# Routed expert outputs added into memory by accumulating indirect DMAs, and the shared expert moved into the routing stage

## The reference

```
scores  = sigmoid(x @ gate_w.T)                       # 2048 tokens, 16 experts
chosen  = top 4 of (scores + expert_bias) per token
weights = scores of the chosen, divided by their sum
routed  = sum over the chosen of weight * swiglu_e(x) # silu(x@wg.T) * (x@wu.T) @ wd.T, inner width 256
shared  = swiglu_shared(x)                            # for every token, weight 1
out     = layernorm(x + routed + shared)
```

## Time and profile before

| | |
|---|---|
| median of 3 runs | 1644.0 us (1643.52 to 1646.49) |
| profiled execution | span 1642.0 us, from its first to its last instruction; no time of its own is given beside it, and the median is 2.0 us above it |
| `route` | about 986 to 1056 us |
| `routed_experts` | about 1056 to 1514 us |
| `combine` | about 1514 to 1642 us |
| PE busy | 1421.5 us, 87% of the span |
| DVE, ACT, POOL busy | 993.8, 659.1 and 271.0 us |

### The profile page before, as it was taken

One profiled execution on the slowest core, in us unless ns is written; L12 is line 12 of the kernel. 1 busy time (PEld: TensorE's weight loads), 2 busy tenths in 40 slices (PEclk: granted clock), 3 DMA queues, 4 the chain that ended last, 5 costly groups with the idle time before them and its releaser, 6 DMA issues. The chain is left out here.

```text
span 1642.0 us, 25753 instructions
## 1 busy us (share of the span) xinstructions
PE 1421.5 (87%) x9093; PEld 1174.7 (72%) x9093; DVE 993.8 (61%) x1677; ACT 659.1 (40%) x1042; POOL 271.0 (17%) x233
## 2 busy tenths in 40 slices
PE   2898998998999758999898985499999999998890
PEld 2665676666766447788787874389999999997770
DVE  4665565565665483444434427777777777775677
ACT  3344233244334223333323314266566655664222
POOL 1002001001000020200102000122222222221762
PEclk9999999999999779999999998589999999999995
DMA  6000000000000032220312004177877878784654
GB/s 268 1 1 26 1 2 27 2 1 1 1 1 1 1 138 83 74 87 16 104 40 77 23 1 142 46 265 276 287 277 275 299 271 292 275 273 178 196 165 142
DMA packets 61589, 190.29 MB, mean 116 GB/s; under 512 B 7112, under 2 KB 7116, under 8 KB 60624
## 3 DMA queue, kind: packets, MB, share of 16 engines
q1 hardware_dynamic: 48880, 147.93, 24.6%
q0 software_dynamic: 12640, 41.43, 8.4%
HBM read 156.30 MB, written 33.03 MB: 115 GB/s over the span
## 5 line engine op out<-in xcount | busy, mean ns | idle before, releaser
L415 PE MATMUL proj_ps<-wqkv,x_sp 128*128 128x384 f32 x768 | 174.5, 362 | 26.4 <-DVE wo L297 26.4
L1510 DVE TENSOR_TENSOR e_w_sp<-e_w_raw,e_w_sp 128x1024 fp32r<-128x1024 f32 x141 | 168.7, 1221 | 18.1 <-ACT e_w_sp L1468 11.3
L952 PE MATMUL c_score_ps<-ct,x_t 128*128 128x402 f32 x768 | 155.4, 364 | 0.0
L952 PEld LDWEIGHTS c_score_ps<-ct,x_t 128*128 128x128 f32 x768 | 149.8, 201 | 6.9 <-issue 6.1
L1454 POOL DMA_INDIRECT e_x_g<-x_rows,e_index x94 | 101.2, 1076 | 323.7 <-DVE e_index L1521 309.1
L415 PEld LDWEIGHTS proj_ps<-wqkv,x_sp 128*128 128x128 f32 x768 | 135.2, 200 | 26.4 <-issue 26.4
L1468 ACT ACTIVATE e_w_sp<-e_w_raw 128x1024 fp32r<-128x1024 f32 x141 | 145.9, 1058 | 16.8 <-DMA e_w_raw<-w_experts 16.6
L992 PE MATMUL c_out_ps<-cr,weigh_t 128*128 128x512 f32 (+1 forms) x624 | 152.5, 399 | 0.0
L1569 PEld LDWEIGHTS e_gate_ps<-e_x_t,e_w_sp 128*128 128x128 f32 x1128 | 140.6, 191 | 5.9 <-DVE e_x_t L1531 1.8
L1569 PE MATMUL e_gate_ps<-e_x_t,e_w_sp 128*128 128x256 f32 x1128 | 142.1, 283 | 1.4 <-DVE e_x_t L1531 1.4
L1569 PE MATMUL e_up_ps<-e_x_t,e_w_sp 128*128 128x256 f32 x1128 | 143.3, 283 | 0.0
(11 more groups left out here) (211 smaller groups left out, 2242.6 us busy)
## 6 DMA issues: line engine op xcount, KB each, us to landing
e_w_raw<-w_experts SPq DMA_DIRECT2D x141, 512.0 KB, 5.6
y_rows<-e_y SPq DMA_DIRECT2D x47, 512.0 KB, 2.9
raw<-ctxT SPq DMA_DIRECT2D x16, 800.5 KB, 4.3
raw<-ctx_rows SPq DMA_DIRECT2D x16, 768.0 KB, 4.8
x_raw<-xT SPq DMA_DIRECT2D x4, 1024.0 KB, 4.8
rows<-x_rows SPq DMA_DIRECT2D x1, 4096.0 KB, 14.2
x_rows<-rows SPq DMA_DIRECT2D x4, 1024.0 KB, 6.2
out<-rows SPq DMA_DIRECT2D x4, 1024.0 KB, 5.3
```

The costliest lines, as they stand in the source:

```text
L415: mm = nc.tensor.matmul(proj_ps[:, tt, 0:GW], x_sp[:, xs, c, tt * P:(tt + 1) * P], wqkv[:, ws, c, hg * GW:(hg + 1) * GW], start=(c == 0 an ...
L952: mm = nc.tensor.matmul(score_ps[:, f, 0:MQ], x1_t[:, xs, c, qt * P:(qt + 1) * P], ct[:, cs, c, f * MQ:(f + 1) * MQ], start=False, stop=(c ...
L1510: nc.vector.tensor_tensor(w_sp[:, par, part, 1, :], w_raw[:, par, part, :], w_sp[:, par, part, 0, :].bitcast(F32), ALU.subtract).then_inc( ...
```

## The change

Four things are done at once.

1. The shared expert moves from `combine` into `route`. Its weights are split part by part between the logits (ACT) and on POOL; it uses the turned rows that `route` has anyway, which are now kept for all 2048 tokens. PE's products are written between the rank matmuls and the marks; DVE adds the down products to `rows` between the marks; POOL makes the low part of `h`. `rows`, now x + shared, are stored by four DMAs of 1 MB to a new tensor `acc` in memory.
2. The weight of each routed pair travels with the row: `x2_rows` gets 16 more columns (2112 bytes a row instead of 2048) that hold the token's weight for each expert, so a gathered tile brings them along. DVE picks the tile's expert by a product with a one-hot row and a reduction (`weigh` of `routed_experts`), and the evictions of the down product multiply by it.
3. `y` of a tile is no longer stored by SP. POOL adds its two halves into `acc` by indirect DMAs with an add (`scatter`). The first half waits until the tile before has landed; empty slots go to 256 spare rows.
4. `combine` goes. `finish_rows` loads `acc` back into `rows` (4 DMAs of 1 MB), does the four norms and stores.

The core of the diff (variable set-up, the removed body of `combine` and index arithmetic are left out):

```diff
 def route(...):
+                sp.wait_ge(weighed, 1)
+                sp.dma_start(x2_rows[0:NT * P, D:D + E].rearrange("(t p) e -> p t e", p=P), weight_row[:, :, :]
+                             ).then_inc(weights_out, 16)
+                for b in range(B):
+                    sp.wait_ge(shared_added, b * TT + TT)
+                    sp.dma_start(acc[b * T:(b + 1) * T, :].rearrange("(t p) d -> p t d", p=P),
+                                 rows[:, b * TT:(b + 1) * TT, :]).then_inc(acc_out, 16)
                 sp.wait_ge(x2_out, B * 16)
+                sp.wait_ge(weights_out, 16)
+                sp.wait_ge(acc_out, B * 16)
...
 # POOL
+                for b in range(B):
+                    pool.wait_ge(h_hi, b + 1)
+                    nc.gpsimd.tensor_tensor(h_sp[:, b % 2, 1, :, :], h_f[:, :, :],
+                                            h_sp[:, b % 2, 0, :, :].bitcast(F32), ALU.subtract).then_inc(h_lo, 1)
...
 # DVE
                 choose()
+                gate_up(0)
                 lay_out()
-                for t in range(NT):
+                for t in range(BEFORE_ADDS):
                     mark(t)
+                gate_up(1)
                 weigh()
+                for t in range(TT):
+                    mark(BEFORE_ADDS + t)
+                    add_shared(t)
+                for t in range(BEFORE_ADDS + TT, BEHIND_UP):
+                    mark(t)
+                gate_up(2)
+                for t in range(BEHIND_UP, NT):
+                    mark(t)
+                    add_shared(TT + t - BEHIND_UP)
+                name_experts()
+                for t in range(TT + NT - BEHIND_UP, 2 * TT):
+                    add_shared(t)
+                find_rows()
+                gate_up(3)
+                for t in range(2 * TT, NT):
+                    add_shared(t)
...
 def routed_experts(...):
 # SP
-                    if exists(n):
-                        sp.wait_ge(y_first, n + 1)
-                        sp.wait_ge(y_second, n + 1)
-                        dst = y_rows[bass.ds(n * SLOTS, SLOTS), :]
-                        sp.dma_start(dst.rearrange("(h p) d -> p h d", p=P), y[:, par, :, :]
-                                     ).then_inc(y_stored[par], 16)
 # POOL
+                def scatter(n, par):
+                    earlier = added(n + 1, 1 - par)
+                    for half, read in ((0, y_first), (1, y_second)):
+                        if half == 0:
+                            if past(n, 1):
+                                pool.wait_ge(*earlier)
+                            pool.wait_ge(aimed, ready)
+                        pool.wait_ge(read, ready)
+                        nc.gpsimd.indirect_dma_start(
+                            acc, bass.IndirectOffsetOnAxis(ap=to_row[:, par, half:half + 1], axis=0),
+                            y[:, par, half, :], None, compute_op=ALU.add
+                        ).then_inc(y_added[par], 16)
+
                 def step(n, par):
-                    m, par = n + 3, 1 - par
-                    ...
+                    if exists(n + 3):
+                        gather(n + 3, 1 - par)
+                    if exists(n):
+                        scatter(n, par)
 # ACT, DVE
-                        nc.scalar.activation(y[:, par, 0, :], down_ps[:, 0, :], ACT.Copy).then_inc(y_first, 1)
+                        nc.scalar.activation(y[:, par, 0, :], down_ps[:, 0, :], ACT.Copy, scale=weight[:, par, 0:1]
+                                             ).then_inc(y_first, 1)
-                        nc.vector.tensor_scalar(y[:, par, 1, :], down_ps[:, 1, :], 1.0, None, ALU.mult
+                        nc.vector.tensor_scalar(y[:, par, 1, :], down_ps[:, 1, :], weight[:, par, 1:2], None, ALU.mult
...
-def combine(nc, sem, rows, w_sp, y_rows, plan, out):
+def finish_rows(nc, sem, rows, acc, out):
+                for b in range(B):
+                    sp.dma_start(rows[:, b * TT:(b + 1) * TT, :],
+                                 acc[b * T:(b + 1) * T, :].rearrange("(t p) d -> p t d", p=P)).then_inc(row_in[b], 16)
```

More of the change, by code:

```diff
@@ L1004, in _, with route @@
                 batch(B - 1, True)
-def route(nc, sem, rows, x2_norm, gate_wT, expert_bias, x2_rows, plan, load_shared, hi_shared):
-    slot_of, weight_of, token_at, expert_at = plan
+def route(nc, sem, rows, x2_norm, gate_wT, expert_bias, shared, x2_rows, acc, plan):
+    weight_row, token_at, expert_at, expert_hot = plan
     _, x2_aggregate, x2_root, x2_normalise, x2_normed = x2_norm
@@ L1331, in _, with routed_experts @@
                     turn_scores(b)
+                front(0, 0)
+                front(0, 1)
                 rank()
-                for t in range(NT):
+                front(1, 0)
+                front(1, 1)
+                for t in range(BEFORE_ADDS):
                     mark(t)
-def routed_experts(nc, sem, w_experts, x2_rows, y_rows, plan, lo_shared):
-    _, _, token_at, expert_at = plan
+                back(0, BEFORE_ADDS, TT)
+                front(2, 0, BEFORE_ADDS + TT, 2)
+                front(2, 1, BEFORE_ADDS + TT + 4, 2)
+                back(1, BEHIND_UP, NT - BEHIND_UP)
+                front(3, 0)
+                front(3, 1)
+                back(2)
+                back(3)
+def routed_experts(nc, sem, w_experts, x2_rows, acc, plan):
+    _, token_at, expert_at, expert_hot = plan
     with ExitStack() as ctx:
@@ L1512, in lo_w, with weigh @@
                                             ).then_inc(w_lo[part], 1)
+                def weigh(m, par):
+                    for half in range(HALVES):
+                        dve.wait_ge(x_in[half][par], times(m, par) * 8)
+                    if past(m, 2):
+                        dve.wait_ge(y_first, m - 1)
+                        dve.wait_ge(y_second, m - 1)
+                    nc.vector.tensor_tensor(weight_in[:, par, :, :], x_g[:, par, :, D:D + E],
+                                            expert_hot[:, bass.ds(m, 1), :].broadcast_to([P, HALVES, E]),
+                                            ALU.mult).then_inc(weight_set, 1)
+                    dve.wait_ge(weight_set, m + 1)
+                    nc.vector.tensor_reduce(weight[:, par, :], weight_in[:, par, :, :], AX, ALU.add
+                                            ).then_inc(weighed, 1)
                 def step(n, par):
+                    if exists(n + 1):
+                        weigh(n + 1, 1 - par)
                     if exists(n + 3):
@@ L1737, in add_shared @@
-                def add_shared(b, so_far, next_x2=None):
-                    dve.wait_ge(added, so_far * TOPK)
-                    for tt in range(TT):
-                        t = b * TT + tt
-                        dve.wait_ge(down_done, t + 1)
-                        nc.vector.tensor_tensor(rows[:, t, :], down_ps[:, t % 2, :], rows[:, t, :],
-                                                ALU.add).then_inc(shared_added, 1)
-                        if next_x2 is not None:
-                            lo_x2(next_x2, tt)
@@ L1749, in norm @@
-                def norm(b):
-                    dve.wait_ge(added, (b + 1) * TT * TOPK)
+                for b in range(B):
+                    dve.wait_ge(row_in[b], 16)
                     for t in range(b * TT, (b + 1) * TT):
-                        dve.wait_ge(shared_added, t + 1)
                         gather(t)
@@ L1868, in experts @@
-        y_rows = nc.dram_tensor("y_rows", (TILES * SLOTS, D), F32, kind="Internal").ap()
-        route(nc, sem, rows, x2_norm, gate_wT, expert_bias, x2_rows, plan, load_shared, hi_shared)
-        routed_experts(nc, sem, w_experts, x2_rows, y_rows, plan, lo_shared)
-        combine(nc, sem, rows, shared_sp, y_rows, plan, out)
+        expert_hot = ctx.enter_context(nc.sbuf_tensor("expert_hot", [P, TILES, E], F32))
+        plan = weight_row, token_at, expert_at, expert_hot
+        x2_rows = nc.dram_tensor("x2_rows", (NT * P, D + E), F32, kind="Internal").ap()
@@ L1874, in decoder_block @@
+        acc = nc.dram_tensor("acc_rows", (NT * P + SLOTS, D), F32, kind="Internal").ap()
+        route(nc, sem, rows, x2_norm, gate_wT, expert_bias, w_experts[0], x2_rows, acc, plan)
+        routed_experts(nc, sem, w_experts, x2_rows, acc, plan)
+        finish_rows(nc, sem, rows, acc, out)
 def decoder_block(nc, xT, x, ctxT, ctx_rows, mask, wqkvT, woT, rope, w_experts, gate_wT, expert_bias, out):
```

443 lines of the change are left out of this document (193 added, 250 removed).

## The result

The changed kernel takes **1688.2 us** (1679.54 to 1689.93, 4 runs) against 1643.9 us (1643.52 to 1646.49, 4 runs) for the kernel before: ratio 1.025, 95% interval 1.023 to 1.027. It is slower, where 1599 us and faster were predicted. The profiled execution has a span of 1686.1 us, against 1642.0.

What follows compares the result with a forecast made beforehand. PE alone was taken to pace `routed_experts`, DVE's chain `route`, and no full engine `combine`. The span 1642.0 + 47 (`route`) + 4 (drain) - 96 (end) = 1597, plus 2 around it, gave 1599 us, range 1590 to 1612.

Steps and rivals of the forecast that it cites:

- The weak step: In `routed_experts`: POOL's scatter chain, 1.25 us plus L, 8.25 us, stays hidden under PE's 9.29 us a tile.
- L: In `routed_experts`: time from the issue of a tile's second scatter half to its landing, taken as 7.0 us.
- Scatters pace the tiles and eat the gain: Rival in `routed_experts`: slower than before from L = 9.0 us; at L = 11.8, 177 us more, 1776 us; chance 0.22.
- Its sign: In the tiles: PE waits for `e_y` evictions and these for landed scatters, with a period above 9.3 us.
- The forecast of 96%: In `routed_experts`: share of queue q0 if an accumulation costs double a gather; 78% if it costs the same.
- +47: In `route`: the stage ends at about 1103.4 instead of 1056.2, +47 us, with bounds +40 to +92.
- The walk: In `route`: step-by-step timing of PE and DVE in the new order, from 1017.1 to about 1103.4 us.
- the longest as under 2.5: In `route`: PE's longest wait found is under 2.5 us, the argument against the clock falling.
- -92: After the tiles' last eviction: the end's -96 us (31.3 against 127.6) with the drain's +4.
- The drain: At the end of `routed_experts`: the store of 2.9 us gives way to a scatter of 7, +4 us.

Runs made afterwards that it cites:

- The experiment on the order alone: Changed kernel with POOL issuing the scatter of tile n-1 behind the gather of tile n+3 instead of ahead: 1628.5 us; over five executions 1629.8 us, ratio 0.991.
- the ring-of-four kernel: Changed kernel with gathered rows in a ring of four instead of two, gathers issued a tile earlier, waits between scatters kept: 1625.7 us.

## Why the prediction was wrong

**The weak step, "hidden if 1.25 + L < 9.29".** This is the step that failed. The sum came to 10.8 us, where the prediction had 8.25, and a cost behind the same wait was left out altogether.
- *The terms of the sum.* From a tile's first half to its second are 2.20 us in the mean, where 1.25 was taken from the spacing of gathers: POOL is busy 1.55 to 2.64 us with the issue of one accumulating scatter. L was taken as 7.0, with about 1 us for the addition because its two reads could run side by side. No run shows how they run; L of the second halves measured 7.63 us in the mean. From a landing to the next start are 0.95 us, where nothing was taken; 0.72 us is the least in any period. With 2.20 and 0.76 us, L would have had to be under 6.3 us to be hidden, and not under 8.0.
- *What is queued behind.* The step named the wait that the change adds, but not what stands behind the scatters on POOL. Those are the next gathers, and they are on PE's path: they left 4.8 us behind their index instead of 0.8, half of it for the issue of two scatters, half for their wait. The experiment on the order alone shows that this causes the loss: 1628.5 us with everything else kept.
- *L as a given.* The median of all landings is 7.9 us in the changed kernel, 6.8 with the other order, and with lighter weight loads the chain is hardly waited for. That the lockstep, in which transfers leave together and the engines then idle at 0.22 to 0.51, is what lengthens it, fits the windows but was not isolated.

Part of the long issues has a visible neighbour. Of the 94 scatters 40 took POOL more than 1.7 us, and every one of these ended 0.3 to 0.4 or 1.4 to 1.5 us behind the end of a DVE subtraction of the expert's weights, as the scatter at 1301.35 did (it ended at 1303.76, DVE at 1303.39). This suggests that DVE holds the issue up; no run took the subtraction away.

```profile
1301.04 2.35 DVE L1705 TENSOR_TENSOR e_w_sp<-e_w_raw,e_w_sp 128x1024 fp32r<-128x1024 f32 x2
```

With the waits spread, the estimate of L itself was fair: a landing of 6.6 to 6.8 us against 7.0, and 9.29 to 9.37 us a tile. That the chain then fits at all is close to luck: 9.4 us in the ring-of-four kernel.

**The rivals.** "Scatters pace the tiles and eat the gain", with a chance of 0.22, is what happened to the time. Its own working had it from L = 9.0 on, a period of 10.25; the period came at 10.75 with L at 7.6, since the other two terms were larger. Its sign was named wrongly too: PE waiting for evictions. PE waited for gathers.

**The traffic.** The forecast of 96% for an accumulation that costs double was about right: with PE at full pace the share is 0.98. The Trainium skill, "Collectives: The Full Stack", Part 3 on the bandwidth ceiling, puts a reduce of the collectives at half the bandwidth of a copy, for its two source reads in one ring; here, by the estimate above, the accumulating scatters take 2.4 times the share of plain ones, somewhat more than that rule. That decides the share, not the time: the engines carry this load at 9.29 us a tile when it comes evenly.

**`route`, +58 instead of +47.** The walk had logits' end at 1017.1; it was 1022.1, as the stage before ended 1.9 us later, the gate weights landed later, and PE's first matmuls ran at the lower clock (granted 0.57 from 997 to 1001, where it had been 1.00). From there to the end of the first four down parts the walk had 35.4 us, and the trace has 39.0. The wait ahead of the third mark was 4.55 us, where the walk had taken the longest as under 2.5, and the slow matmuls behind it cost some 3 us more. Two us of that wait are POOL's subtraction, a term that the walk put at nothing: with it on DVE the wait is 2.53 us. What is left is DVE's queue (product, weights, mark), as moving the third mark shows: 0.76 us. The smaller waits between marks (0.80, 0.87, 1.42) were left out as well. The rest went as walked: 11.2 us a batch of gate and up, 5.6 us of down.

**The end, -85 instead of -92.** Norms, scalings and the last store cost what was estimated (last scaling at 1678.38 + 2.92, end at 1686.1). What cost more was the way there:

```profile
1646.28 1.55 POOL L1641 DMA_INDIRECT acc_rows<-e_y,e_to_row  x1 [0.30 <-issue]
1660.46 2.47 DVE L561 BATCH_NORM_STATS2 norm_stats<-rows 128x6 f32<-128x512 f32 x4 [20.19 <-DMA rows<-acc_rows]
```

The last scatter starts 6.0 us behind the last eviction (1640.27), since its first half too waits for the tile before; the first norm starts 20.2 us behind that eviction. The drain was priced at one landing of 7 us, but it is that wait and then a landing, of 4.9 us now that the engines are free. Another 3.6 us pass before the first load leaves at 1654.80, and the load takes 5.7 us to the norm, where 5.0 were taken.

## What to carry to other kernels

When a change puts a wait on an in-order engine, list what stands behind it and who needs that, and let what the critical engine needs go first: two lines of order were worth 58 us here, about as much as a deeper ring. A chain of landings is to be priced with its issue times, with the time from a landing to the next start, and with the landing that the resulting traffic gives, not that of the kernel before. And look for stretches in which the DMA engines idle between bursts: behind a mean share of 0.85 there were stretches at 0.22, and the same work ran at 0.98 once the order had changed.

## What the runs showed of the hardware

- An accumulating indirect DMA of 256 KB: POOL is busy 1.63 us (1.55 to 2.64) with it against 0.99 for a plain one, it lands in 6.6 to 7.9 us against 2.9, and takes 2.4 times the DMA share (an estimate from three traces). On POOL a scatter that waits for a landing starts 0.72 to 0.76 us behind it (46 of 46 in the ring-of-four kernel).
- While POOL runs a subtraction of 1024 columns from SBUF (2.4 us), DVE operations of 16 or 512 columns that read SBUF alone take until about its end: 2.89 us instead of 0.81, 2.65 instead of 0.64, and a later mark 2.41. DVE's additions of 512 columns with one input from PSUM took their usual 0.69 us beside such a subtraction (at 1100.32 and 1101.71, POOL from 1099.90 to 1102.31). On DVE the same subtraction takes about 1.2 us.
- PE's granted clock fell after waits of 4.55 and 2.53 us, and in one run after two of 1.14 and 0.45 us close together; the group of matmuls behind them took up to 1.8 times its usual time.
